# Routing stage of an attention and mixture-of-experts kernel: constants made earlier, expert tables built beside the digit search, selection in four passes, list steps written out

## What is computed

```python
x = hidden_states.reshape(-1, H)              # 8192 tokens
logits = x @ Wr + br                          # 8 experts
top_vals, top_idx = jax.lax.top_k(logits, 2)
w_flat = jax.nn.softmax(top_vals, axis=-1).reshape(-1)
cap = max(int(math.ceil(N / E * CF)), 1)      # 1280 places an expert
key_mat = jnp.where(flat_idx[None, :] == jnp.arange(E)[:, None], w_flat[None, :], NEG)
kv, ki = jax.lax.top_k(key_mat, cap)          # each expert keeps its best 1280
valid = kv > NEG / 2
tok = flat_tok[ki]
gate = jnp.where(valid, w_flat[ki], 0.0)
xe = x[tok]
h1 = jax.nn.gelu(jnp.einsum('ech,ehf->ecf', xe, W1) + b1[:, None, :], approximate=False)
y = jnp.einsum('ecf,efh->ech', h1, W2) + b2[:, None, :]
out = jnp.zeros_like(x).at[tok.reshape(-1)].add((y * gate[..., None]).reshape(-1, H))
```

## Time and profile before

| | us |
|---|---|
| median of 3 runs | 1386.81 (1386.51 to 1387.3) |
| the profiled execution, its own time | 1389.0 |
| its span | 1387.2 |
| PE busy | 1163.1 (84%) |
| DVE busy | 995.6 (72%) |
| POOL busy | 971.6 (70%) |
| ACT busy | 754.9 (54%) |

### The profile page before, as it was taken

The page is one execution under the profiler, slowest core; times in us unless marked ns, Lnnn a source line. Parts: engine busy times, 40 slices in busy tenths (PEclk is TensorE's granted clock), DMA queues, the critical chain, the costliest instruction groups (busy, mean ns, idle before and its releaser), DMA issues. The chain is left out here.

```text
span 1387.2 us, 23869 instructions
## 1 busy us (share of the span) xinstructions
PE 1163.1 (84%) x5973; PEld 783.3 (56%) x5974; DVE 995.6 (72%) x2205; ACT 754.9 (54%) x1482; POOL 971.6 (70%) x1081
## 2 busy tenths in 40 slices
PE   7899999999999999999999999999931164979500
PEld 5556566665656666565666656565431163979500
DVE  3888687777767777776777778676457884777596
ACT  4565666666576666657666665665413233444144
POOL 3386978878697887869788786978743066545268
PEclk9999999999999999999999999999965555999855
DMA  4000101011010101101010100001032013232474
GB/s 149 16 18 16 58 6 62 16 47 46 15 53 8 62 16 46 46 15 53 9 62 16 46 32 17 32 17 46 31 129 24 18 43 88 43 95 43 87 253 166
DMA packets 68477, 70.89 MB, mean 51 GB/s; under 512 B 12912, under 2 KB 64032, under 8 KB 68272
## 3 DMA queue, kind: packets, MB, share of 16 engines
q1 hardware_dynamic: 46800, 47.18, 10.7%
q10 hardware_dynamic: 16896, 16.78, 3.6%
q0 software_dynamic: 4704, 6.11, 2.9%
HBM read 40.35 MB, written 29.45 MB: 50 GB/s over the span
## 5 line engine op out<-in xcount | busy, mean ns | idle before, releaser
L559 ACT ACTIVATE PF<-PS 128x512 f32<-128x512 f32 x512 | 298.3, 595 | 256.8 <-PE PS L929 247.6
L821 DVE TENSOR_REDUCE NMAX<-PS 128x1 f32<-128x512 f32 x512 | 342.4, 682 | 88.0 <-PE PS L938 84.5
L472 POOL TENSOR_TENSOR SF<-SF,PF 128x512 f32<-128x512 f32 x252 | 322.0, 1300 | 14.7 <-ACT PF L559 14.5
L1010 PE MATMUL PS<-PF,V 128*64 128x512 f32 x1024 | 248.0, 605 | 0.0
L928 PE MATMUL PS<-Q,K 128*128 128x512 f32 x512 | 222.3, 434 | 2.8 <-ACT PF L559 2.8
L938 PE MATMUL PS<-K,Q 128*128 128x512 f32 x512 | 205.5, 403 | 10.6 <-DVE NMAX L821 10.2
L929 PE MATMUL PS<-Q,K 128*128 128x512 f32 x512 | 201.4, 393 | 0.0
L578 ACT ACTIVATE Q<-PS 64x512 fp32r<-64x512 f32 x256 | 151.5, 592 | 48.3 <-PE PS L94 43.3
L469 POOL TENSOR_TENSOR SF<-PF 128x512 f32<-128x512 f32 x126 | 162.0, 1301 | 19.6 <-ACT PF L559 19.6
L500 POOL TENSOR_TENSOR XL<-XF,XH 128x512 fp32r<-128x512 f32 x63 | 82.6, 1312 | 128.5 <-ACT XH L633 128.4
L928 PEld LDWEIGHTS PS<-Q,K 128*128 128x128 f32 x512 | 96.5, 188 | 120.5 <-ACT PF L559 54.6
(11 more groups left out here) (327 smaller groups left out, 2519.7 us busy)
## 6 DMA issues: line engine op xcount, KB each, us to landing
X<-in_L_attn_x SPq DMA_DIRECT2D x16, 512.0 KB, 3.4
MODB<-mod_rows SPq DMA_DIRECT2D x16, 512.0 KB, 3.7
h_rows<-H ACTq DMA_DIRECT2D x16, 512.0 KB, 3.0
acc_rows<-H ACTq DMA_DIRECT2D x16, 512.0 KB, 4.1
out_x<-X SPq DMA_DIRECT2D x16, 512.0 KB, 2.9
A<-acc_rows SPq DMA_DIRECT2D x15, 512.0 KB, 8.8
W1F<-in_L_ffn_W SPq DMA_DIRECT2D x3, 1024.0 KB, 4.9
W2F<-in_L_ffn_W SPq DMA_DIRECT2D x3, 1024.0 KB
```

What stands on the lines that cost most here:

```text
L472: s_sum.done(pool.tensor_tensor(total, total, tile, ALU.add))
L559: s_exp.done(act.activation(PF[:, u % 8, :], st_bank(u), ACT.Exp))
L821: s_mred.done(dve.tensor_reduce(NMAX[:, p % 2, r:r + 1], mx_bank(u), AX.X, ALU.max, negate=True))
L1010: last = pe.matmul(num_bank(p)[odd * R:(odd + 1) * R, :], V1[:, vp, c, :], PF[:, k % 8, :], start=(c == 0), stop=(c == TC - 1))
```

## The change

Four things are done.

1. The constants of `route` are made by POOL inside `attention`, ahead of slot 20 of the pipeline's round -1 (`routing_constants`, on a semaphore of its own), and three small ones (`LOWER`, `ECOLI`, `ECOL`) by DVE at slot 20 of sequence 0. In `route` POOL makes five fills, and DVE waits for those before it writes `KEY`.
2. The expert tables are built from the first digit's data: an expert's number of assigned keys comes from one ACT instruction (`SGN` on `HI` with its sum `ASG`), and ACT, POOL and PE make the tables beside the digits. DVE copies `INFO` in digit 8. POOL's first scatter stands behind its part of that.
3. The selection has no `GT` on DVE: ACT gives the sign against the threshold (`SGN`), DVE `EQT`, `SCAN`, one combination (`RANK`), and one comparison with sum (`SEL`).
4. The list steps are written out, without loop registers. They read the number row from a copy in PSUM (`iot_ps`, written by ACT), and only the first of a token's two places is converted before them; the second is worked out by DVE between steps 0 to 5 (`second`).

The diff, cut to its core:

```diff
@@ attention, POOL
+                link(pool.iota(RANK8[:, :], pattern=[[-1, E]], base=E, channel_multiplier=0, **f32))
+                link(pool.iota(ECOLI, pattern=[[0, 1]], base=0, channel_multiplier=1))
+                link(pool.iota(m["PIDX"][:, :], pattern=[[0, 1]], base=0, channel_multiplier=1, **f32))
+                link(pool.tensor_scalar(m["LOW8"][:, :], m["PIDX"][:, :], float(E), None, ALU.is_lt))
...
+                for j, blocks in enumerate((0, 0, 2, 3, 4)):
+                    link(pool.memset(NBLEV[:, j:j + 1], float(2 * blocks * BLK - NT)))
...
             def body(b, par):
                 for n in range(UNITS):
+                    if isinstance(b, int) and (b, n) == (-1, 20):
+                        routing_constants()
@@ attention, DVE, same_expert
+                mask(dve.scalar_tensor_tensor(out=m["LOWER"][:, :], in0=DIFF, scalar=float(P), in1=m["SAME"][:, :],
+                                              op0=ALU.is_gt, op1=ALU.mult))
+                dve.wait_ge(s_rc, 2)
+                mask(dve.tensor_scalar(ECOLI, ECOLI, E - 1, None, ALU.bitwise_and))
+                mask(dve.tensor_scalar(m["ECOL"][:, :], ECOLI, float(CAP), float(-1 - BIG), ALU.mult, ALU.add))
@@ route, POOL
...
+        pool.memset(ONES[:, :], 1.0).then_inc(s_pool, 1)
...
+        pool.wait_ge(s_nba, 1)
+        pool.tensor_scalar(OVER[:, :], NBLEV[:, :], TOTAL[:, :], LOW8[:, :], ALU.is_lt, ALU.mult).then_inc(s_nbp, 1)
+        pool.wait_ge(s_nba, 3)
+        pool.tensor_scalar(PICK[:, :], IOT[:, 0:E], PRIOR[:, 0:1], OVER[:, 0:1], ALU.is_equal, ALU.mult).then_inc(s_nbp, 1)
+        pool.tensor_scalar(LASTB[:, :], BLOCKS[:, :], -1.0, None, ALU.add).then_inc(s_nbp, 1)
...
         first_scatter(pool, m)
@@ route, ACT
+        act.activation(iot_ps, IOT[:, :], ACT.Copy).then_inc(s_iot, 1)
         act.wait_ge(s_dd, 1)
         act.activation(EX[:, :], DEN[:, :], ACT.Exp).then_inc(s_exp, 1)
+        act.wait_ge(s_split, 1)
+        act.wait_ge(s_pool, POOL_CONSTS)
+        act.activation(SGN[:, :], HI[:, :], ACT.Sign, bias=ONES[:, 0:1], accum_out=ASG[:, :]).then_inc(s_asg, 1)
...
+            if d == 1:
+                act.wait_ge(s_nbt, 1)
+                act.activation(TOTAL[:, :], asg_ps, ACT.Copy).then_inc(s_nba, 1)
+            if d == 2:
+                act.wait_ge(s_nbt, 2)
+                act.activation(PRIOR[:, :], prior_ps, ACT.Copy, accum_out=FIRSTB[:, :]).then_inc(s_nba, 1)
+                act.activation(JUNKB[:, :], OVER[:, :], ACT.Copy, accum_out=BLOCKS[:, :]).then_inc(s_nba, 1)
...
+        act.activation(SGN[:, :], LOW[:, :], ACT.Sign, bias=CAND[:, NDIG % 2, 0:1], scale=-1.0, accum_out=CNT[:, 1:2]).then_inc(s_sgn, 1)
@@ route, PE
+        pe.wait_ge(s_asg, 1)
+        pe.matmul(asg_ps, SAME[:, :], ASG[:, :], start=True, stop=True).then_inc(s_nbt, 1)
...
+            if d == 1:
+                pe.wait_ge(s_pool, BEFORE_AT)
+                pe.wait_ge(s_nbp, 1)
+                pe.wait_ge(s_nba, 1)
+                pe.matmul(prior_ps, BEFORE[:, :], OVER[:, :], start=True, stop=True).then_inc(s_nbt, 1)
+            if d == 5:
+                pe.wait_ge(s_nbp, 8)
+                pe.wait_ge(s_nba, 3)
+                pe.matmul(table_ps, ONES[:, :], TABLE[:, :], start=True, stop=True).then_inc(s_nbt, 1)
@@ route, DVE
-        dve.wait_ge(s_pool, 1)
...
-        dve.wait_ge(s_pool, POOL_CONSTS)
...
+            if d == 8:
+                dve.wait_ge(s_nbt, 3)
+                dve.tensor_copy(m["INFO"][:, :], table_ps[0:1, :]).then_inc(s_info, 1)
...
-        link(dve.tensor_scalar(GT[:, :], LOW[:, :], thr, None, ALU.is_gt, ALU.add, accum_out=CNT[:, 1:2]))
...
+        dve.wait_ge(s_sgn, 1)
+        link(dve.tensor_tensor(CNT[:, 3:4], CNT[:, 2:3], CNT[:, 1:2], ALU.add))
...
+        link(dve.scalar_tensor_tensor(out=RANK[:, :], in0=SGN[:, :], scalar=FAR, in1=SCAN[:, :], op0=ALU.mult, op1=ALU.add))
...
+        link(dve.tensor_scalar(SEL[:, :], RANK[:, :], CNT[:, 4:5], None, ALU.is_le, ALU.add, accum_out=CNT[:, 5:6]))
...
+        to_integers(0)
+        to_places(0)
+        to_floats(0)
+        dve.wait_ge(s_iot, 1)
+        for j in range(STEPS):
+            dve.wait_ge(s_mm, j + 1)
+            dve.tensor_tensor(OE[:, j % 2, :, :], iot_ps[:, 0:SLOTC].unsqueeze(1).broadcast_to([P, RING, SLOTC]),
+                              af[:, j * RING:(j + 1) * RING].unsqueeze(2).broadcast_to([P, RING, SLOTC]), ALU.is_equal).then_inc(s_oe, 1)
+            dve.tensor_tensor(OB[:, j % 2, :, :], iot_ps.unsqueeze(1).broadcast_to([P, RING, P]),
+                              bf[:, j * RING:(j + 1) * RING].unsqueeze(2).broadcast_to([P, RING, P]), ALU.is_equal).then_inc(s_ob, 1)
+            second(j)
```

More of the change, by code:

```diff
@@ L113, in build_program @@
         m["LOGITS"] = sb("LOGITS", [P, NCH, E])
-        m["SAME"] = sb("SAME", [P, P])
+        m["SAME"], m["LOWER"] = sb("SAME", [P, P]), sb("LOWER", [P, P])
+        for k, shape in (("RANK8", [P, E]), ("IOT", [P, P]), ("SPARE", [P, E * CAP // P]), ("TOK1", [P, 2, NCH]), ("ECOL", [P, 1]),
+                         ("PIDX", [P, 1]), ("LOW8", [P, 1]), ("NEED", [P, BASE - 1]), ("NBLEV", [P, NBLV]),
+                         ("LEVEL", [P, NDIG, BASE]), ("STEP", [P, NDIG, BASE]), ("MOVE", [P, NDIG, BASE])):
+            m[k] = sb(k, shape)
         with ExitStack() as attn:
@@ L1054, in route @@
     M1, M2, I1, I2, EX, W1, W2, DEN = (sb(x, [P, NCH]) for x in ("M1", "M2", "I1", "I2", "EX", "W1", "W2", "DENr"))
-    RANK8 = sb("RANK8", [P, E])
-    HI, LO, LOW, GT, EQT, SEL, SCAN, DST, ZT = (sb(x, [P, T]) for x in ("HI", "LO", "LOW", "GT", "EQT", "SEL", "SCAN", "DST", "ZT"))
+    HI, LO, LOW, SGN, EQT, RANK, SEL, SCAN, DST, ZT = (
+        sb(x, [P, T]) for x in ("HI", "LO", "LOW", "SGN", "EQT", "RANK", "SEL", "SCAN", "DST", "ZT"))
     BITS, JUNK = sb("BITS", [P, 2, T], U32), [sb(f"JUNK{j}", [P, T]) for j in range(BASE - 1)]
-    SAME, LOWER, ONES, DIFF = m["SAME"], sb("LOWER", [P, P]), sb("ONES", [P, P]), sb("DIFFr", [P, P], I32)
-    LEVEL, STEP, MOVE = (sb(x, [P, NDIG, BASE]) for x in ("LEVEL", "STEP", "MOVE"))
-    SIGN, COUNT, MID2, NEED = sb("SIGN", [P, BASE]), sb("COUNT", [P, BASE]), sb("MID2", [P, 2, BASE]), sb("NEED", [P, BASE - 1])
+    SAME, LOWER, ONES, BEFORE = m["SAME"], m["LOWER"], sb("ONES", [P, P]), sb("BEFORE", [P, P])
+    RANK8, IOT, SPARE, TOK1, ECOL, PIDX, LOW8 = (m[x] for x in ("RANK8", "IOT", "SPARE", "TOK1", "ECOL", "PIDX", "LOW8"))
+    LEVEL, STEP, MOVE, NEED, NBLEV = (m[x] for x in ("LEVEL", "STEP", "MOVE", "NEED", "NBLEV"))
     CAND, CNTS, NEXTC = sb("CAND", [P, 2, BASE]), sb("CNTS", [P, BASE - 1]), sb("NEXTC", [P, BASE])
     PASS, DIG = sb("PASS", [P, BASE - 1]), sb("DIG", [P, 1])
[L1068 to L1076, removed]
+    CNT, SUMS = sb("CNT", [P, 8]), sb("SUMS", [P, 2])
+    D12 = sb("D12", [P, 2, NCH])
+    DI, AI, BI = (sb(x, [P, 2, NCH], U32) for x in ("DI", "AI", "BI"))
+    AF, BF = sb("AF", [P, 2, NCH]), sb("BF", [P, 2, NCH])
     OB, OE, OA = sb("OB", [P, 2, RING, P], F32R), sb("OE", [P, 2, RING, SLOTC]), sb("OA", [P, 2, RING, SLOTC], F32R)
@@ L1148, in _ @@
[L1148 to L1157 removed]
+        pool.wait_ge(s_pool, ZEROS)
@@ L1334, in _ @@
         dve.wait_ge(s_sum, NDIG + 2)
[L1335 to L1336 removed]
+        link(dve.tensor_tensor(CNT[:, 6:7], ECOL[:, :], off_ps, ALU.add))
+        link(dve.scalar_tensor_tensor(out=DST[:, :], in0=SCAN[:, :], scalar=CNT[:, 6:7], in1=SEL[:, :],
                                       op0=ALU.add, op1=ALU.mult))
[L1339 removed]
```

257 lines of the change are left out of this document (118 added, 139 removed).

## The result

| | before | after |
| --- | --- | --- |
| median (us), runs in one session | 1387.05 (1386.51 to 1389.3, 4 runs) | 1364.92 (1363.85 to 1365.12, 4 runs) |
| profiled execution, span | 1389.0, 1387.2 | 1363.85, 1362.1 |

The ratio is 0.9831, 95% interval 0.9818 to 0.9845: faster by 23.4 us (21.5 to 25.2), where 19.7 were forecast. The two medians of the table are 22.1 apart; both figures are above the forecast. The cause of the larger part of the gain was named rightly; its size was not, and one part of it was not named.

The account below looks back on a forecast made before the run. No engine was always busy; routing was bound by DVE's waits and chains and DVE-POOL turns. 0.2 + 3.4 + 0.1 + 4.15 + 2.8 + 2.9 + 6.1 = 19.7 off 1386.8 gave 1367.1 us; range 1364 to 1372.5.

Parts of the forecast that it names:

- Who takes turns: List steps: DVE and POOL exclude each other when DVE reads two SBUF inputs, which sets the 2.53 us period.
- The turns stay: Rival, list steps: they keep 2.53 us because the second SBUF input isn't what is shared; 1373.2 us, chance 0.12.
- PSUM reads cost nothing: List steps: OE and OB reading the number row from PSUM keep 0.82 and 1.21 us.
- The clock: Rival, list: PE's clock rises from the 1.2 GHz level, the ring falls below DVE's 1.88; 1364.7 us, chance 0.08.
- Slower: steps starve for instructions: Rival, list: written-out steps wait for instructions, 26 us lost if each second step pays; 1393.5 us, chance 0.03.
- Constants, tables, places: Routing: BITS no longer waits for POOL, 3.4 us; tables leave DVE's chain after DST, 4.15; shorter place work, 2.9.
- part 3: Selection, from the threshold to PE's transposes: a shorter chain, 6.8 instead of 9.6 us, gain 2.8.
- part 5's 6.1: List steps: 2.05 us each in the steady part instead of 2.53, list 37.2 instead of 43.3 us, gain 6.1.
- The small terms: Routing: taking LOWER out of the digits gives 0.1 us; KEY is not held up; small terms within 1 us.
- the attention's end must stay: Attention: added POOL and DVE instructions fit into idle time at no cost, so its end stays at 1030 us.

Follow-up runs that it names:

- experiment 1: The changed kernel with OE and OB reading the number row from SBUF (IOT) again; 1371.24 us, one run; list 44.11 instead of 36.36 us.
- experiment 4: The changed kernel, once with the old selection (threshold to transposes 8.00, not 6.82 us), once with DVE's old table chain added (transposes to reduction 5.18, not 1.15).
- Experiment 2: The changed kernel with second places made before the list: 1367.61 us; with its list steps also in a hardware loop over pairs: 1367.39 us; one run each.
- experiment 6: The kernel before with tiny DVE instructions added in the attention: one 1387.07 us, two 1389.66, three and a wait 1385.33 (ratio 0.9984).

## Why the prediction was right, and where it was not

**Who takes turns** was right and is shown by experiment 1: with one SBUF input too many, DVE and POOL exclude each other, and the number row's place alone moves a step from 2.53 to 1.99. The rule of the Trainium skill (SBUF — State Buffer, Who interferes with whom) held in both directions. *The turns stay* is refuted.

**PSUM reads cost nothing** was right: `OE` 0.82 and `OB` 1.21 from either place. The rule of the Trainium skill weighed against it (VectorE: DVE Perf Modes, the TRN2 errata section) doesn't show here; by it 32 instructions would have lost an estimated 2 us.

**The clock** didn't rise: 0.50 with PE busy 19.0 of 20 us, and 15.95 of 16 with three buffers. *Slower: steps starve for instructions* is refuted too. POOL starts 0.08 after `OE`, and PE 0.06 after `OB` (1111.91 against 1110.64 + 1.21).

**Constants, tables, places** came out within 0.15 us each: 3.37 against 3.4, 4.16 against 4.15, 3.03 against 2.9. In part 3 the sum of 2.8 was right because it was taken between two points of the timeline; that it was the selection's gain was wrong (experiment 4: the selection gave 1.18, the rest came from tables and `ECOL`).

**The step that failed first: part 5's 6.1.** It measured 6.95. Steps 0 to 5 took 14.12 us (14.2 forecast) and the end 4.46 (4.5); the nine steps after that took 17.78, 1.98 each, where 2.05 was taken, which makes 0.67 of the 0.85. The ring had been worked out right, 3.99 for two steps against 3.98 measured. The forecast then moved up towards the 4.26 with the present loop's hand-offs. Experiment 2 puts the loop at 4.17, so that bound was fair for a loop and wrong for written-out code, although the forecast had the digits' hand-offs of 0.04 to 0.06 in hand.

**The small terms.** `HI`'s cast (0.3 less, with POOL's fills no longer beside it) and the keys (0.17) were taken as nothing; together with `LOWER` that is 0.53 against 0.1. POOL's constants took 14.3 us in the attention (29.89 to 44.2) where 18.2 were summed up; they fit either way.

**The step that failed second: "the attention's end must stay".** The constants did cost nothing there, as argued. But "no cost" was taken to mean "no effect", and DVE's stop of 1.84 us, visible in the trace of before, got no term. Three instructions and a wait ahead of it took it off the path: 1.35 us in the interval, and 2.2 (1.0 to 3.5) in the runs of experiment 6. That the kernel with no routing edit at all gains this shows that it is none of the change's purposes.

**The sum.** 20.98 of routing and 1.35 of the stop make 22.3, against 22.1 between the medians and 23.4 (21.5 to 25.2) by the ratio. So nothing that is clear of noise is missing, but the agreement with the medians to 0.2 is luck: starts differ by 3 us and ends by 2.5 from one execution to the next. The start's 3 us in the profiled pair isn't part of the sum.

## What to carry to other kernels

When two engines' instructions grow while they overlap and each shrinks alone, write the period as a sum of turns before anything else; moving one shared constant into PSUM, so that the elementwise instruction reads one SBUF operand, gave more here than writing out 16 steps (7.75 us in experiment 1 against 1.76 in experiment 2). Work out what bounds the steps next (here the ring, with DVE 0.12 behind it), and use the hand-offs of code in the form that the new code has. Before saying that instructions added in idle time change nothing, look for idle stretches marked "issue" behind a loop's exit in the same engine's stream: inserting instructions ahead can move such a stop onto the path or off it (the interval went from 60.27 to 62.94 us here), and a gain of that size isn't evidence for the edit that brought it.

## What the runs showed that was not expected

- DVE's stream stops once for 1.84 to 3.15 us of idle time in straight code after a loop's exit; with one and with two instructions added ahead it falls one and two instructions earlier, and with three and a wait it isn't seen. ACT has such an idle time too, 1.41 to 1.71 us marked "issue" ahead of `H<-X,NB,NY` at 865 to 871 us in all fourteen profiles; what it costs wasn't tested.
- The start of one program differs by up to 3 us between executions (first `SF` on POOL from 47.27 to 50.26 with the same attention code), of which PE's fall to the 1.2 GHz level near 40 us makes up to 0.6; without the fall it was 48.03 and 48.14.
- POOL's 128x400 product takes 0.86 alone and 1.67 to 1.77 in turns. DVE's 128x640 comparison in turns takes 0.91 in the looped steps and 1.17 in the written-out ones, for the same period of 2.53.
- PE's clock stays at the 1.2 GHz level through the list even with PE busy 15.95 of 16 us (products of 80 columns, granted clock 0.50).
- A hardware loop over pairs costs about 0.1 us a step against written-out code at these hand-offs (4.17 against 3.98 for two).
